# Projections stage: turns as 64-row tile pairs, four product banks, one query copy, no waiting additions

## The chip, the cores and the metric

One core of one Trainium2 chip runs the whole program. The metric is device time in microseconds (us) from the first to the last instruction; lower is better. The kernel before takes 2472.25 us (median of 3 runs, 2471.01 to 2472.43). TensorE is PE in the profile (PEld its weight loads), VectorE DVE, ScalarE ACT, GpSimd POOL, SyncE SP.

## The reference, cut to what matters

Two residual blocks on x (8 images, 256 channels, 64 by 64 pixels, float32). The change lies in the second one, in its projection `qkv` and in the sum `vk` over all pixels.

```python
x = x + _L0_conv_ref(_gn(x), ...)             # window mixing
# second block, on _gn(x):
qkv = einsum('bchw,oc->bohw', x, w_qkv)       # 768 output channels
y = conv5x5(qkv); y = conv1x1(y)              # a second set of 768
mqkv = concatenate([qkv, y]).reshape(B, -1, 24, N)
q, k, v = relu(first 8), relu(next 8), last 8 # per head
v = pad(v, ones row)
vk = einsum('bhdn,bhen->bhde', v, k)
out = einsum('bhde,bhen->bhdn', vk, q); out = out[:-1] / out[-1:]
x = x + batch_norm(einsum('bchw,oc->bohw', out, w_proj))
```

## The kernel before, in words

Four stages follow one another: window mixing, projections, convolved heads, output. Only `projections` is changed. It takes the images one by one, each in 8 chunks of 512 pixels (`n` from 0 to 7; 64 chunks in all). Images 0, 1, 6 and 7 are written out with constant wait values; images 2 to 5 run in a loop of two rounds, two images a round, and wait on values from registers (`over_image_pairs`). Below, "written-out" and "looped" chunks are these two kinds, 32 each.

A chunk on TensorE (`body` under `@block.tensor`):

- `product(b, n, j)` for j = 0 to 5 makes one tile of 128 output channels from six 128 by 128 by 512 matmuls (three float32r terms for two channel halves). j = 0 and 2 are the two key tiles, 1 and 3 the two value tiles, 4 and 5 the two query tiles. The products go round three PSUM banks, `o_ps[:, j % 3]`.
- `turn(b, n, u)` turns key tile and value tile of pair u (u = 0 after product 2, u = 1 after product 4) so that pixels lie on partitions: four 128 by 128 transposes each, keys into bank 0 of `t_ps`, values into bank 1. It first waits for four semaphores: that ScalarE has emptied the banks (`k_turned`, `v_turned`), and that the tiles lie in SBUF (`kv_ready`, `kv_ready_v`).
- `sum_vk(b, n, u)` for both u at the chunk's end adds value times key over the pixels: 16 small matmuls for each u, on tiles of 128 rows by 32 columns.
- In chunk n = 5, `means` and `variances` of the next image's normalization stand between the products.

The other engines in a chunk:

- ScalarE: `key(0)` copies product 0 out to `kv`; half of the next chunk's normalization; `key(1)`; `turned(0)`; the other half and the cast `xh`; the first query tile (`qw`, after product 4); `turned(1)`. A `turned` is two copies of 512 columns, `kT` and `vT`.
- VectorE: `value(n, 0)` copies product 1 out; pair differences into `stage` (`keys_values`); differences of the chunk before's queries; `value(n, 1)`; differences; `split` (the low part `xl` of the next chunk); the second query tile (L1314, after product 5); in chunks 1 to 4 a quarter of the next image's moments (`moments`), in chunk 4 also `gather`, whose result `means` waits for. The wait for product 1 is followed by three more semaphores (`cells_free`).
- GpSimd: for keys and values of each u and for queries `edge` and a copy into `stage`, then two ReLU passes of the queries into `qs`. After its waits and ahead of each `edge` it does a 128 by 1 addition into `tick` (`pause`), and so before `border`, a memset.
- SyncE stores `stage` and `qs` to DRAM as they get ready.

Semaphores that TensorE waits for before a product: j = 0 the second value copy and the first query copy of the chunk before; 1 the first query copy; 2 the second; 3 this chunk's first key copy; 4 the first value copy; 5 the second key copy.

In the next stage, `convolved_heads`, `turn` (L1572) is already made of 32-row tiles, in four banks, after small matmuls and ahead of a product. Its rows are read below for what such tiles cost.

Of the kernel before, what the change touches and what calls it, by code (L numbers as in the profile page):

```python
# [25 lines left out]
ALU = mybir.AluOpType  # L26
# [710 lines left out]
def projections(nc, K, x1_dram, qkv_dram, qr_dram, w_pw, bn_in, taps_dram, sorted_dram):  # L737
# [3 lines left out]
    with ExitStack() as ctx:  # L741
# [25 lines left out]
        vT = sb("vT", [P, 2, 4, NSQ, VS])  # L767
        tick = sb("ptick", [P, 4 * NCH])
# [6 lines left out]
        o_ps = psum("o_ps", [P, 3, 512])  # L775
        t_ps = psum("pt_ps", [P, 2, 512])
        vk_ps = psum("vk_ps", [P, 2, 512])
# [13 lines left out]
        kv_ready_v, q_ready_v = sem("kv_ready_v"), sem("q_ready_v")  # L791
# [5 lines left out]
        counted = sem("p_counted")  # L797

# [80 lines left out]
        def cells_free(eng, g):  # L879

            at_least(eng, t_full, 4 * (g - 1))
            at_least(eng, kv_diff, 2 * (g - 1))
            at_least(eng, kv_odd, 2 * (g - 1))
# [7 lines left out]
        def _(pool):  # L891
            pool.memset(vT[:, :, :, :, SQ:VS], 1.0).then_inc(zeroed, 1)

            def body(i, last_body):
                for par in range(2):
                    b = 2 * i + par

                    def pause(k, n):

                        k = NCH * k + n  # L900
                        pool.tensor_tensor(tick[:, k:k + 1], K["ident"][:, 0:1], K["ident"][:, 1:2], ALU.add)

                    def border(n):

                        row = NB * (1 - n // 4)
                        keys_values_free(pool, b, n)
                        queries_free(pool, b, n)
                        pause(0, n)
                        pool.memset(stage[:, n % 2, :, :, :, row, :].rearrange("p t a k x -> p (t a) k x"), 0.0)

                    def edge(buf, t0, j0, n):

                        if n % 2:
                            pool.tensor_scalar(staged(j0, n, 0, 0, 1), every_second(buf, t0, n, 0, 1), -1.0, None, ALU.mult)
                        else:
                            pool.tensor_copy(staged(j0, n, 1, HALF - 1, HALF), every_second(buf, t0, n, NB - 1, 1))

                    def keys_values(n, u):
# [4 lines left out]
                        pause(1 + u, n)  # L923
                        edge(kv, 2 * u, 2 * u, n)
                        pool.tensor_copy(staged(2 * u, n, 2), every_second(kv, 2 * u, n, 1 - n % 2)).then_inc(kv_odd, 1)

                    def queries(n, end=False):
                        g = NCH * b + n
                        pool.wait_ge(q_ready, g + 1)
                        pool.wait_ge(q_ready_v, g + 1)  # L930
                        queries_free(pool, b, n)
                        at_least(pool, K["qr_stored"][n % 2], 32 * (4 * b + n // 2))
                        pause(3, n)
# [8 lines left out]
                    for n in range(NCH):  # L942
                        if n % 4 < 2:
                            border(n)
# [8 lines left out]
        def _(act):  # L953
# [79 lines left out]
            def body(i, last_body):  # L1033
                for par in range(2):
                    b = 2 * i + par
                    for n in range(NCH):
# [5 lines left out]
                        def key(u):  # L1042
# [3 lines left out]
                            act.activation(kv[:, n % 2, 2 * u, :], o_ps[:, (2 * u) % 3, :], ACT.Copy).then_inc(kv_ready, 1)  # L1046

                        def turned(u):
                            act.wait_ge(t_full, 4 * g + 2 * u + 1)
                            at_least(act, vk_full, g)  # L1050
                            act.activation(kT[:, u, :, :].rearrange("p a c -> p (a c)"), t_ps[:, 0, :], ACT.Relu)\
                                .then_inc(k_turned, 1)
                            act.wait_ge(t_full, 4 * g + 2 * u + 2)
                            act.activation(vT[:, u, :, :, 0:SQ].rearrange("p a q c -> p (a q) c"),
                                           t_ps[:, 1, :].rearrange("p (a c) -> p a c", c=SQ), ACT.Copy).then_inc(v_turned, 1)
# [18 lines left out]
                        act.wait_ge(o_full, o0 + 5)  # L1074
                        queries_read(act, g)
                        act.activation(qw[:, n % 2, 0, :], o_ps[:, 1, :], ACT.Copy).then_inc(q_ready, 1)
                        turned(1)
                        if last_body and par == 1 and n == NCH - 1:
                            act.wait_ge(q_ready, g + 1)
                            act.wait_ge(q_ready_v, g + 1)  # L1080
# [18 lines left out]
        def _(pe):  # L1099
# [8 lines left out]
            pe.wait_ge(zeroed, 1)  # L1108

            def product(b, n, j):  # L1110
# [5 lines left out]
                if j == 0:  # L1116
                    at_least(pe, kv_ready_v, 2 * (NCH * b + n))
                    at_least(pe, q_ready, NCH * b + n)
                if j == 1:
                    at_least(pe, q_ready, NCH * b + n)  # L1120
# [1116 lines left out]
```

## Time and profile before

| | us |
|---|---|
| median of 3 runs | 2472.25 |
| lowest, highest | 2471.01, 2472.43 |
| span of the profiled execution | 2473.8 |
| first and last product matmul of the stage (L1132) | 266.9, 999.3 |

The profiled execution lies 1.5 us (0.06%) above the median. Starts are in us from the start of the span. A matmul's recorded time is its latency; matmuls are pipelined, so what a sequence costs is read from start to start.

### The profile page before, as it was taken

To read this page: it belongs to the slowest core of one execution; us is meant where nothing else is said; L and a number is where in the kernel's file an instruction comes from. 1 tells how busy PE (TensorE), PEld (TensorE's weight loads), DVE (VectorE), ACT (ScalarE), POOL (GpSimd) and SP (SyncE) were. 2 spreads that over 40 slices of the span, in tenths; PEclk is the share of its full clock that TensorE was granted. 3 is DMA by queue.
4 is the path that set the end of the run, shared out by engine and by line. 5 is a ranking of instruction groups with operands and counts; after the bars stand their busy time and mean duration, and the time that the engine had idled before them with its cause. 6 is when DMAs were issued, how large, how long until landed. Compare 5 with 4: busy or idle time off the path is not lost. (4 is left out here: it accounts for less than half of the span.)

```text
span 2473.8 us, 66794 instructions
## 1 busy us (share of the span) xinstructions
PE 2359.6 (95%) x25485; PEld 1881.3 (76%) x25485; DVE 1994.9 (81%) x2653; ACT 1495.6 (60%) x1864; POOL 1099.8 (44%) x1476
## 2 busy tenths in 40 slices
PE   5999799999999999799999999999999889999998
PEld 5889688877777887577888888888888656666666
DVE  7887688878788877778888888888888588888775
ACT  5777566666566666566776776677767434433442
POOL 7722387887787878200000000000000068888887
PEclk9999899999999999899999999999999999999999
DMA  7874689988988989988888888888888777777774
GB/s 285 336 301 173 208 295 344 329 293 314 316 288 323 344 299 302 253 196 207 209 209 208 209 210 207 210 208 209 207 208 210 228 243 280 275 275 271 271 272 136
DMA packets 300973, 628.38 MB, mean 254 GB/s; under 512 B 50784, under 2 KB 252256, under 8 KB 291552
## 3 DMA queue, kind: packets, MB, share of 16 engines
q1 hardware_dynamic: 295072, 590.38, 77.5%
q10 hardware_dynamic: 4688, 31.63, 3.6%
q0 software_dynamic: 1008, 3.67, 0.4%
q8 instruction: 125, 2.05, 0.3%
q14 instruction: 80, 0.66, 0.1%
HBM read 327.81 MB, written 300.94 MB: 254 GB/s over the span
## 5 line engine op out<-in xcount | busy, mean ns | idle before, releaser
L1562 PE MATMUL c_ps<-dh,wh 128*128 128x512 f32 x1152 | 465.3, 404 | 15.8 <-DVE wl L1712 9.9
L1477 ACT ACTIVATE dh<-image 128x1632 fp32r<-128x1632 f32 x192 | 301.5, 1570 | 269.9 <-PE c_ps L1562 254.8
L1562 PE MATMUL c_ps<-dh,wl 128*128 128x512 f32 x1152 | 456.4, 396 | 0.0
L1562 PE MATMUL c_ps<-dl,wh 128*128 128x512 f32 x1152 | 454.6, 395 | 1.6 <-issue 1.6
L1921 POOL TENSOR_TENSOR ql<-image,qh 128x1024 fp32r<-128x1024 f32 x1 | 2.4, 2359 | 967.8 <-DVE ql L2152 967.8
L1670 DVE TENSOR_TENSOR dl<-image,dh 128x1632 fp32r<-128x1632 f32 x192 | 356.3, 1856 | 73.9 <-ACT dh L1477 73.9
L1132 PE MATMUL o_ps<-xh,wqh 128*128 128x512 f32 x768 | 319.2, 416 | 11.3 <-issue 8.4
L1909 POOL TENSOR_TENSOR ql<-image,qh 128x1024 fp32r<-128x1024 f32 x126 | 300.9, 2413 | 10.7 <-ACT qh L1940 10.7
L1132 PE MATMUL o_ps<-xl,wqh 128*128 128x512 f32 x768 | 303.5, 395 | 0.0
L1132 PE MATMUL o_ps<-xh,wql 128*128 128x512 f32 x768 | 301.9, 393 | 0.0
L1562 PEld LDWEIGHTS c_ps<-dh,wh 128*128 128x128 f32 x1152 | 218.5, 190 | 68.6 <-DVE wl L1712 10.0
L1562 PEld LDWEIGHTS c_ps<-dl,wh 128*128 128x128 f32 x1152 | 218.2, 189 | 53.8 <-issue 1.3
L1562 PEld LDWEIGHTS c_ps<-dh,wl 128*128 128x128 f32 x1152 | 218.7, 190 | 46.1
L939 POOL TENSOR_SCALAR qs<-qw 128x512 f32<-128x512 f32 x126 | 239.1, 1913 | 0.0
L1046 ACT ACTIVATE kv<-o_ps 128x512 f32<-128x512 f32 x128 | 76.9, 601 | 255.8 <-PE o_ps L1132 246.0
L1961 ACT ACTIVATE zs<-z_ps,bn_shift 128x512 f32<-128x512 f32 x64 | 44.0, 687 | 278.2 <-PE z_ps L2048 278.2
L2048 PE MATMUL z_ps<-qh,fh 128*128 128x512 f32 x512 | 207.9, 406 | 3.1 <-issue 1.7
L2048 PE MATMUL z_ps<-qh,fl 128*128 128x512 f32 x512 | 200.1, 391 | 0.0
L2048 PE MATMUL z_ps<-ql,fh 128*128 128x512 f32 x512 | 199.8, 390 | 0.0
L1277 DVE COPY kv<-o_ps 128x512 f32<-128x512 f32 x128 | 87.9, 687 | 124.2 <-PE o_ps L1132 123.4
L973 ACT ACTIVATE xn<-image,p_nb,p_sc 128x512 f32<-128x512 f32 (+2 forms) x160 | 175.6, 1120 | 7.6 <-PEq L255 7.6
L1132 PEld LDWEIGHTS o_ps<-xh,wqh 128*128 128x128 f32 x768 | 145.8, 190 | 39.8 <-issue 14.2
(212 smaller groups left out, 5107.8 us busy)
## 6 DMA issues: line engine op xcount, KB each, us to landing
qkv_scratch<-stage SPq DMA_DIRECT2D x384, 408.0 KB, 4.7
image<-qkv_scratch SPq DMA_DIRECT2D x189, 816.0 KB, 6.3
yq_scratch<-qy SPq DMA_DIRECT2D x64, 512.0 KB, 6.7
image<-qr_scratch SPq DMA_DIRECT2D x128, 256.0 KB, 6.1
image<-yq_scratch SPq DMA_DIRECT2D x128, 256.0 KB, 5.3
ox<-x_scratch SPq DMA_DIRECT2D x8, 4096.0 KB, 15.3
qr_scratch<-qs SPq DMA_DIRECT2D x126, 256.0 KB, 3.6
out<-ox SPq DMA_DIRECT2D x7, 4096.0 KB, 12.7
```

Of the source, the lines that this page charges most:

```text
L939: last = pool.tensor_scalar(qs[:, n % 2, t, :], qw[:, n % 2, t, :], 0.0, None, ALU.max)
L973: last = act.activation(dst[:, :, to:to + rows, :], src[:, :, of:of + rows, :], ACT.Identity, bias=T["nb"][:, ct:ct + 1], scale=T["sc"][:, ...
L1046: act.activation(kv[:, n % 2, 2 * u, :], o_ps[:, (2 * u) % 3, :], ACT.Copy).then_inc(kv_ready, 1)
L1132: last = pe.matmul(o_ps[:, j % 3, :], w[:, ct, P * t:P * t + P], xx[:, n % 2, ct, :], start=(k == 0), stop=(k == 5))
L1277: dve.tensor_copy(kv[:, n % 2, 2 * u + 1, :], o_ps[:, (2 * u + 1) % 3, :]).then_inc(kv_ready_v, 1)
L1477: act.activation(dh[kind][:, :], raw[kind], ACT.Copy).then_inc(hi_ready, 1)
L1562: last = pe.matmul(c_ps[:, m, :], w[hp][:, kind, part, o:o + P], cells[:, :, HALF * dy:HALF * dy + HALF * NB], start=(k == 0), stop=(k == 5))
L1670: dve.tensor_tensor(dl[kind][:, :], raw[kind], dh[kind][:, :].bitcast(F32), ALU.subtract)\
L1909: pool.tensor_tensor(two_of(ql, n, tp), two(n, tp), two_of(qh, n, tp).bitcast(F32), ALU.subtract)\
L1921: pool.tensor_tensor(two_of(ql, 0, 1), two(0, 1), two_of(qh, 0, 1).bitcast(F32), ALU.subtract).then_inc(ql_ready, 2)
L1961: act.activation(zs[:, :], z_ps[:, 1, :], ACT.Identity, bias=bn["shift"][:, 1:2]).then_inc(z_taken, 1)
L2048: last = pe.matmul(z_ps[:, o, :], w[par][:, t, P * o:P * o + P], d, start=(m == 0), stop=(m == 3 * KT - 1))
```

## The change

`turn` becomes, for keys and values and each of four blocks, two transposes of 64 rows each: rows 0 to 63 into bank 0 and rows 64 to 127 into bank 1, so that keys take the first 256 columns of both banks and values the second 256. It raises `t_full` once, at its end, instead of after the keys and again after the values. Its four waits (`turn_ready`) move ahead of the last matmul of the product in front of it. `kT` and `vT` are read out with the two banks as one more dimension.

The products go round four banks, `(6n + j) % 4`; the two sums `vk` share one bank instead of two. ScalarE copies both query tiles in one activation of 1,024 columns after product 5 and after `turned(1)`; VectorE's copy of the second one is gone, and with it `q_ready_v` in all waits. Waits before products: j = 0 the second key copy of the chunk before, 1 the second value copy, 2 and 3 the query copy; 4 the first key copy of this chunk, 5 the first value copy. `pause` is gone on GpSimd; `edge` becomes a two-input operation with a zero; `border` comes after the first `edge`.

```diff
-            act.wait_ge(t_full, 4 * g + 2 * u + 1)
+            act.wait_ge(t_full, 2 * g + u + 1)
...
-        act.wait_ge(o_full, o0 + 5)
+        turned(1)
+        act.wait_ge(o_full, o0 + 6)
         queries_read(act, g)
-        act.activation(qw[:, n % 2, 0, :], o_ps[:, 1, :], ACT.Copy).then_inc(q_ready, 1)
-        turned(1)
+        act.activation(qw[:, n % 2, :, :], o_ps[:, bank(n, 4):bank(n, 4) + 2, :], ACT.Copy).then_inc(q_ready, 1)
...
+def product(b, n, j, before_last=None):
...
                 for w, xx in ((wh, xh), (wl, xh), (wh, xl)):
+                    if k == 5 and before_last:
+                        before_last()
...
-    for s in range(2):
+    for s, out in ((0, kt_ps), (1, vt_ps)):
         for a in range(4):
-            last = pe.transpose(t_ps[:, s, P * a:P * a + P], kv[:, n % 2, 2 * u + s, P * a:P * a + P], K["ident"][:, :])
-        last.then_inc(t_full, 1)
+            for r in range(2):
+                rows = slice(HALF_ROWS * r, HALF_ROWS * r + HALF_ROWS)
+                last = pe.transpose(out[:, r, HALF_ROWS * a:HALF_ROWS * a + HALF_ROWS],
+                                    kv[rows, n % 2, 2 * u + s, P * a:P * a + P], K["ident"][rows, rows])
+    last.then_inc(t_full, 1)
...
-                        product(b, n, 2)
-                        turn(b, n, 0)
+                        product(b, n, 2, lambda: turn_ready(b, n, 0))
+                        turn(n, 0)
...
-                        product(b, n, 4)
+                        product(b, n, 4, lambda: turn_ready(b, n, 1))
...
-                        dve.wait_ge(o_full, QT * g + 6)
-                        queries_read(dve, g)
-                        dve.tensor_copy(qw[:, n % 2, 1, :], o_ps[:, 2, :]).then_inc(q_ready_v, 1)
```

## Rows read from the trace of the kernel before

**Rows 1.** The page: each engine's busy time, share of the span and instructions.
```profile
PE 2359.6 (95%) x25485; PEld 1881.3 (76%) x25485; DVE 1994.9 (81%) x2653; ACT 1495.6 (60%) x1864; POOL 1099.8 (44%) x1476
```

**Rows 2.** Groups, 300 to 960 us: shapes, count, busy us, mean ns, idle before.
```profile
L1146 PE MATMUL pt_ps<-ident,kv 128*128 128x128 f32 x928 | 121.6, 274 | 5.3 <-DVE kv L1277 4.9
...
L901 POOL TENSOR_TENSOR ptick<-ident 128x1 f32<-128x1 f32 x204 | 87.4, 429 | 142.3 <-issue 63.1 <-DMA qkv_scratch<-stage 59.0 <-DVE kv L1277 20.2
...
L984 ACT ACTIVATE xh<-xn 128x1024 fp32r<-128x1024 f32 x57 | 60.5, 1061 | 1.9
...
L1314 DVE COPY qw<-o_ps 128x512 f32<-128x512 f32 x58 | 39.6, 683 | 2.9 <-PE o_ps L1132 2.4
```

**Rows 3.** Timeline of PE, one looped chunk: start, length, what, idle before.
```profile
610.64 0.47 PE L1132 MATMUL o_ps<-xh,wqh 128*128 128x512 f32 x1
...
614.39 0.39 PE L1132 MATMUL o_ps<-xh,wql 128*128 128x512 f32 x1
614.62 0.39 PE L1132 MATMUL o_ps<-xl,wqh 128*128 128x512 f32 x1
614.85 1.03 PE L1146 MATMUL pt_ps<-ident,kv 128*128 128x128 f32 x8
615.64 0.47 PE L1132 MATMUL o_ps<-xh,wqh 128*128 128x512 f32 x1
615.95 0.39 PE L1132 MATMUL o_ps<-xh,wql 128*128 128x512 f32 x1
...
618.26 0.39 PE L1132 MATMUL o_ps<-xl,wqh 128*128 128x512 f32 x1
...
620.86 0.76 PE L1158 MATMUL vk_ps<-vT,kT 128*32 128x33 f32 x64
621.82 0.47 PE L1132 MATMUL o_ps<-xh,wqh 128*128 128x512 f32 x1 [0.20 <-issue]
```

**Rows 4.** Timeline of PE in the convolved heads: product, small sums, 32-row turns, product.
```profile
1403.87 0.40 PE L1562 MATMUL c_ps<-dl,wh 128*128 128x512 f32 x1
1404.20 0.77 PE L1590 MATMUL yvk_ps<-yvT,ykT 128*32 128x33 f32 x64
1404.90 0.69 PE L1572 MATMUL yt_ps<-ident,vy 32*128 32x32 f32 x32
1405.42 0.67 PE L1572 MATMUL yt_ps<-ident,ky 32*128 32x32 f32 x32
1406.01 0.51 PE L1562 MATMUL c_ps<-dh,wh 128*128 128x512 f32 x1
1406.36 0.39 PE L1562 MATMUL c_ps<-dh,wl 128*128 128x512 f32 x1
```

**Rows 5.** Timeline of DVE, the value copies of the looped chunk in rows 3.
```profile
613.87 0.69 DVE L1277 COPY kv<-o_ps 128x512 f32<-128x512 f32 x1 [3.28 <-PE o_ps L1132]
...
617.66 0.68 DVE L1277 COPY kv<-o_ps 128x512 f32<-128x512 f32 x1
```

**Rows 6.** Timeline of PE, a written-out chunk: last matmul of product 2, chunk's end.
```profile
378.96 0.40 PE L1132 MATMUL o_ps<-xl,wqh 128*128 128x512 f32 x1
...
385.18 0.76 PE L1158 MATMUL vk_ps<-vT,kT 128*32 128x33 f32 x64
385.90 0.47 PE L1132 MATMUL o_ps<-xh,wqh 128*128 128x512 f32 x1
```

**Rows 7.** Timeline of DVE, the first value copy of that written-out chunk.
```profile
378.02 0.69 DVE L1277 COPY kv<-o_ps 128x512 f32<-128x512 f32 x1 [2.96 <-PE o_ps L1132]
```

**Rows 8.** Timeline of DVE: a value copy that comes late.
```profile
759.41 0.68 DVE L1277 COPY kv<-o_ps 128x512 f32<-128x512 f32 x1
```

**Rows 9.** Timeline of PE: the turn that waited for that copy.
```profile
760.24 1.07 PE L1146 MATMUL pt_ps<-ident,kv 128*128 128x128 f32 x8 [0.20 <-DVE kv L1277]
```

**Rows 10.** Timeline of PE, chunk 5: last matmul of product 1, then the means.
```profile
601.24 0.39 PE L1132 MATMUL o_ps<-xl,wqh 128*128 128x512 f32 x1
...
601.84 0.38 PE L161 MATMUL pstat_ps<-pmv,gavg 128*128 128x2 f32 x2 [0.22 <-DVE pmv L120]
```

More of the change, by code:

```diff
@@ L797, in projections, with bank @@
         counted = sem("p_counted")
+        def bank(n, j):
+            return (QT * n + j) % NO
         def image(i, par):
@@ L879, in cells_free @@
         def cells_free(eng, g):
-            at_least(eng, t_full, 4 * (g - 1))
+            at_least(eng, t_full, 2 * (g - 1))
             at_least(eng, kv_diff, 2 * (g - 1))
@@ L891, in _ @@
         def _(pool):
-            pool.memset(vT[:, :, :, :, SQ:VS], 1.0).then_inc(zeroed, 1)
+            pool.memset(zero[:, :], 0.0).then_inc(zeroed, 1)
+            pool.memset(vT[:, :, :, :, :, SQ:VS], 1.0).then_inc(zeroed, 1)
+            pool.wait_ge(zeroed, 2)
+            none = zero[:, :].unsqueeze(1).unsqueeze(2).broadcast_to([P, 4, NB, 1])
             def body(i, last_body):
@@ L922, in keys_values @@
                         keys_values_free(pool, b, n)
-                        pause(1 + u, n)
+                        if u == 0 and n % 4 < 2:
+                            queries_free(pool, b, n)
                         edge(kv, 2 * u, 2 * u, n)
+                        if u == 0 and n % 4 < 2:
+                            border(n)
                         pool.tensor_copy(staged(2 * u, n, 2), every_second(kv, 2 * u, n, 1 - n % 2)).then_inc(kv_odd, 1)
@@ L1107, in _ @@
                 last.then_inc(w_turned, 1)
-            pe.wait_ge(zeroed, 1)
-            def product(b, n, j):
+            pe.wait_ge(zeroed, 2)
+            def product(b, n, j, before_last=None):
                 t = TILES[j]
@@ L1131, in product @@
                     for w, xx in ((wh, xh), (wl, xh), (wh, xl)):
-                        last = pe.matmul(o_ps[:, j % 3, :], w[:, ct, P * t:P * t + P], xx[:, n % 2, ct, :],
+                        if k == 5 and before_last:
+                            before_last()
+                        last = pe.matmul(o_ps[:, bank(n, j), :], w[:, ct, P * t:P * t + P], xx[:, n % 2, ct, :],
                                          start=(k == 0), stop=(k == 5))
@@ L1135, in product, with turn_ready @@
                 last.then_inc(o_full, 1)
-            def turn(b, n, u):
+            def turn_ready(b, n, u):
                 at_least(pe, k_turned, 2 * (NCH * b + n) + u)
@@ L1143, in turn @@
                 pe.wait_ge(kv_ready_v, 2 * (NCH * b + n) + u + 1)
-                for s in range(2):
+            def turn(n, u):
+                for s, out in ((0, kt_ps), (1, vt_ps)):
                     for a in range(4):
-                        last = pe.transpose(t_ps[:, s, P * a:P * a + P], kv[:, n % 2, 2 * u + s, P * a:P * a + P],
-                                            K["ident"][:, :])
-                    last.then_inc(t_full, 1)
+                        for r in range(2):
[3 more added lines that the diff above has]
+                last.then_inc(t_full, 1)
             def sum_vk(b, n, u):
@@ L1157, in sum_vk @@
                         ch = slice(SQ * q, SQ * q + SQ)
-                        last = pe.matmul(vk_ps[ch, u, 0:VS], kT[:, u, a, ch], vT[:, u, a, q, :],
-                                         start=(n == 0 and a == 0), stop=(n == NCH - 1 and a == 3))
+                        last = pe.matmul(vk_ps[ch, u, 0:VS], kT[:, u, a, ch], vT[:, u, q // 2, a, q % 2, :],
+                                         start=(n == 0 and u == 0 and a == 0), stop=(n == NCH - 1 and u == 1 and a == 3))
                 if u == 1:
@@ L1276, in value @@
                             cells_free(dve, g)
-                        dve.tensor_copy(kv[:, n % 2, 2 * u + 1, :], o_ps[:, (2 * u + 1) % 3, :]).then_inc(kv_ready_v, 1)
+                        dve.tensor_copy(kv[:, n % 2, 2 * u + 1, :], o_ps[:, bank(n, 2 * u + 1), :]).then_inc(kv_ready_v, 1)
                     def keys_values(n, u):
```

56 lines of the change are left out of this document (22 added, 34 removed).

## The prediction

> **What bounds the kernel now.** I read the page first: TensorE is busy 95% of the span and no other engine over 81% [rows 1]. Busy time of pipelined matmuls says little, so I went to TensorE's timeline in the changed stage, from start to start. The reader is to see that nothing waits: product matmuls follow each other 0.23 us apart (614.39 to 614.62), the turn follows the last of them at the same 0.23, the next product follows the turn, and the chunk closes with the sums [rows 3]. One looped chunk is 11.18 us (from the first product's start at 610.64 to the next chunk's at 621.82). So in this stage each nanosecond that TensorE's sequence gets longer or shorter counts 64 times, and a saving on ScalarE, VectorE or GpSimd counts only where TensorE waits for it. Those places are few: idle time before all turns is 5.3 us in 660 us [rows 2], a fifth of a microsecond at a looped chunk's start marked "issue" [rows 3], and the means of chunk 5 [rows 10].
>
> **Part 1, the turn.** Before: the last product matmul starts at 614.62, the turn's first transpose at 614.85, the next product at 615.64, its second matmul at 615.95 [rows 3]. That is 1.33 us from the last matmul to the second one; without a turn two steps of 0.23 would lie there, so a turn costs 0.87. Eight transposes in 0.79 us are some 0.109 each (the last one's start to the product is about 0.03).
>
> After: the nearest rows are the turns of the convolved heads, with 32-row tiles [rows 4]. They show three prices.
> (a) Into a tiled stretch: from the last product matmul to the first tiled one 0.33 us (1403.87 to 1404.20), 0.10 more than the 0.23 inside a product. Nothing was waited for.
> (b) A block: the two turns start at 1404.90 and 1405.42, so 8 blocks take 0.52 us, 0.065 each as four 32-row tiles with 32 moving columns, against 0.109 as one tile of 128 rows with 128.
> (c) Out of it: the second turn's last block then starts at 1405.42 + 7 x 0.065 = 1405.87; the product starts 0.14 later (1406.01), against 0.03 after full transposes, and its second matmul 0.35 after that (1406.36), against 0.31. Together 0.15 more.
>
> A pair of 64-row tiles moves 64 columns. A straight line between the two rows of (b) gives 0.080 for it; its ends are 0.065 (the weight loads set the pace and the columns cost nothing) and 0.109 (the halves gain nothing). I take 0.080, since the pair differs from both rows in nothing but rows and columns per tile. Seven steps of 0.080 instead of 0.109 save 0.20; the drain of 64 columns instead of 32 takes about 0.01 more. A turn changes by +0.10 + 0.15 + 0.01 - 0.20 = +0.06, to the rows' hundredths; the start differences round up, and I take +0.05. For 128 turns **+6 us**. With 0.065 it is -0.05 a turn or -7 us, with 0.109 +0.26 or +33.
>
> The Trainium skill, "TensorEngine Tiling (Array Packing)", section Key Properties, says that changing the tiling mode drains TensorE; it speaks against short tiled turns between long products. (a) and (c), 0.25 a turn, agree with it; without it the same turns would give -25 us (rival 4).
>
> **Part 2, the waits moved ahead of a product's last matmul.** Queued behind them on TensorE are that matmul, the turn and everything after; the other engines all live on these products. The wait that ends last is VectorE's value copy. Where it holds a turn up, the turn starts 0.15 us after the copy's end: the copy ends at 760.09 and the turn starts at 760.24 [rows 8, 9]. A matmul held like that also pays its weight load in the open, 0.08 us (0.31 instead of 0.23 after a turn [rows 3]). So the last matmul is late by copy's end + 0.23 - its present start, if that is positive.
> Looped chunks, u = 0: the copy ends at 613.87 + 0.69 = 614.56, the matmul starts at 614.62 [rows 3, 5]: late by 0.17. 26 of the 28 looped chunks other than n = 5 look alike (copy's end -0.06 to +0.04 around the matmul's start); in chunk 5 the means leave room. 24 x 0.17 and 0.25 in the four first chunks are 5.1 us. The copy's own waits get one value fewer to work out (`t_full` now has the same as its neighbours), which may give up to 0.09 of it back; I take half, -1.3 us.
> Looped, u = 1: the copy ends at 618.34, the matmul starts at 618.26 [rows 3, 5], late by 0.31; but by then TensorE is 0.23 behind (0.17 and one turn), and VectorE's chain hangs on product 1, so about 0.08 is left in even chunks and nothing in odd ones: 1 us.
> Written-out chunks: the copy ends at 378.71, the matmul starts at 378.96 [rows 6, 7]: 0.25 of room for 0.23, so nothing, but with 0.02 to spare. Sum **+5 us**, with bounds 0 and +11 (written-out turns late by 0.05 each, +3; no relief at u = 1, 0.31 instead of 0.08 in twelve chunks, +3).
>
> **Part 3, the chunk's start.** From the sums to the product takes 0.96 us in the looped chunk (620.86 to 621.82, idle for "issue") and 0.72 in a written-out one [rows 3, 6]: 0.24 of register and wait instructions in TensorE's queue. Product 0 loses one of two waits. The 0.24 holds two or three such steps in the open, so one takes some 0.1 (an estimate): 32 x -0.1 = **-3 us**, between 0 and -6.
>
> **Part 4, the query copy.** VectorE loses 0.68 us a chunk [rows 2]. Its only use is chunk 4, where the moments come that much earlier: the means start 0.60 us after the last matmul instead of 0.23 [rows 10], and 0.37 of waiting goes, in seven chunks: **-2.6 us**. ScalarE's copy grows from 512 to 1,024 columns, 1.06 us by its cast of that size [rows 2]. Behind its wait for product 5 stand the next chunk's `key(0)` (due some 2.7 us later, two products' length) and the normalization; TensorE's product 2 and VectorE's differences need the queries later still. Hidden. `turned(1)` starts after the whole turn instead of after half, but without a query copy in front; two copies of 512 columns take about one of 1,024, so they end some 2 us after the turn starts, and the sums come 2.4 us after it (618.26 + 0.23 to 620.86 [rows 3]). Hidden, with 0.4 to spare.
>
> **Part 5, the rest.** Four banks: no product waits for a bank today, so nothing. The shared bank of the sums: nothing. GpSimd loses 204 additions of 0.43 us in 660 us [rows 2] and pays two-input edges; TensorE's releasers in these groups are VectorE and its own issue, not GpSimd [rows 2, 3], and SyncE gets its stores earlier. 59 of the 142 us of idle time before them are waiting for stores, which start no sooner by much: 0, with -3 as a bound for the few chunks where VectorE waits for a store too. The stage's end loses a pause of 0.43 and gains 0.38 of copy: 0.
>
> **Sum.** +6 + 5 - 3 - 2.6 = about +5 us. The profiled span of 2473.8 stands 1.5 over the median; the sum is made on differences and goes onto the median: **2477 us**.
>
> **Rivals.** (1) Faster: the weight loads alone set the pace of a pair. The rows cannot part load from columns in the 0.065; then the turns give -7 instead of +6, and with the copies 0.09 earlier part 2 gives +4: 2472 - 7 + 4 - 6 = 2463. It decides if a block takes under 0.073, where a turn costs what it does now. Against it: from 32 to 128 columns a block grows by 0.044. Chance 0.18.
> (2) The pair gains nothing, 0.109 a block: 2472 + 33 + 5 - 6 = 2504. Against it: four 32-row tiles do overlap [rows 4]. 0.07. The Trainium skill, "TensorE: Matmul & The Clock Gate", section LDWEIGHTS (loading the stationary operand), says that a load takes as long for 32 rows as for 128; if the sixteen loads of a turn went one after another, that rule would give this case.
> (3) Slower by the moved waits: they bite in the written-out images too, and u = 1 gets no relief, +11 instead of +5: 2483. For it: only 0.02 us of room [rows 6, 7]. 0.15.
> (4) The change does not do what it says: the 64-row turns run as before in the array's full mode, no switch is paid, but blocks still take 0.080: a turn loses 0.2, 2472 - 25 + 5 - 6 = 2446. Against it: [rows 4]. 0.05.
>
> **How the numbers follow.** My forecast's case has 0.55, its own range 2471 to 2483. The range is 2461 to 2488: it takes in rivals 1 and 3 and the bounds of parts 2 to 5, and leaves out 2 and 4 (0.12). A measurement of this kernel tells about 0.2% (4.9 us) from no change; the forecast lies at that edge, so its 0.55 is 0.27 slower, 0.27 same, 0.01 faster. Rival 1 adds 0.15 faster and 0.03 same, rival 2 0.07 slower, rival 3 0.14 slower and 0.01 same, rival 4 0.05 faster. Rounded: faster 0.21, same 0.31, slower 0.48.
>
> **What would show it.** In the profile after: last product matmul to first transpose 0.32 to 0.33; blocks 0.08 apart; 0.15 and 0.34 out of the turn; in looped chunks a gap of 0.40 instead of 0.23 ahead of product 2's last matmul, none in written-out ones; sums to product shorter by 0.1 in looped chunks; means 0.23 after the last matmul. I am wrong if written-out chunks get shorter (turn) or looped ones don't get longer by more than the written-out ones do (waits).

## The result, and the profile after

The changed kernel takes 2477.88 us (median; 2474.38 to 2482.05) against 2471.54 of the kernel before on the same chip: 1.0025 times, 95% interval 1.0015 to 1.0035, so some 6 us slower. The forecast was 2477. That the total came out is luck: the turns were forecast to cost 6 us and gain 6, and what the moved waits and GpSimd's program cost beyond the forecast makes up for that.

The page's first line of the changed kernel (as [rows 1]):

```profile
PE 2364.4 (96%) x26509; PEld 1842.6 (74%) x26509; DVE 1977.6 (80%) x2589; ACT 1545.0 (62%) x1864; POOL 1015.7 (41%) x1253
```

VectorE and GpSimd do less, ScalarE a little more, and TensorE's loads take less: sixteen half tiles for eight whole ones. Nothing of that is the time. TensorE's timeline of the same looped chunk as in [rows 3] (start, length, what):

```profile
613.07 0.49 PE L1131 MATMUL o_ps<-xh,wqh 128*128 128x512 f32 x1
...
616.81 0.39 PE L1131 MATMUL o_ps<-xh,wql 128*128 128x512 f32 x1
617.03 0.39 PE L1131 MATMUL o_ps<-xl,wqh 128*128 128x512 f32 x1
617.36 0.71 PE L1148 MATMUL pt_ps<-ident,kv 64*128 64x64 f32 x16
...
618.34 0.39 PE L1131 MATMUL o_ps<-xh,wql 128*128 128x512 f32 x1
...
620.41 0.39 PE L1131 MATMUL o_ps<-xh,wql 128*128 128x512 f32 x1
620.87 0.47 PE L1131 MATMUL o_ps<-xl,wqh 128*128 128x512 f32 x1
621.27 0.71 PE L1148 MATMUL pt_ps<-ident,kv 64*128 64x64 f32 x16
...
624.34 0.49 PE L1131 MATMUL o_ps<-xh,wqh 128*128 128x512 f32 x1
```

The chunk takes 11.27 us (613.07 to 624.34) against 11.18. At the first turn (u = 0) nothing waits: the last matmul stands 0.22 after the one ahead of it (616.81 to 617.03), the turn follows at 0.33, and from last matmul to second one of the next product it is 1.31 against 1.33. At the second (u = 1) the last matmul stands 0.46 behind (620.41 to 620.87): it waits for VectorE's second value copy. Before it stood 0.23 behind. The turn then follows after 0.40 instead of 0.32.

This is the pattern of the whole stage. Summed over the 64 chunks, start to start: the gaps ahead of product 4's last matmul give 18.0 us; against them stand the two turns with what is around them, -10.1 (part of it waits that stood behind the matmul before), the means -3.3 and the chunk starts -2.6. From the first product to the last chunk's start the stage takes 725.1 us against 720.5. Over all 64 chunks, to the last product's last matmul, it is 7.0 longer, so these four, +2.0 together, are not all: the other 5 are spread over steps inside products and the sums. Of them 1.4 are seven steps of the last chunk, at 0.43 us instead of 0.23: TensorE's granted clock is 0.57 there (994 to 998 us), for most of it the lower of its two levels (1.2 GHz), behind sums in which TensorE had sat idle for 1.62 us. In the kernel before it is 1.00 in that chunk.

Why the second value copy is late shows on VectorE. A written-out chunk (n = 1 of image 1, whose first value copy is [rows 7]) in the timeline of the kernel before, VectorE and then GpSimd:

```profile
378.81 0.63 DVE L1230 TENSOR_TENSOR stage<-kv 128x448 f32<-128x448 f32 x1
379.35 0.69 DVE L1232 TENSOR_TENSOR stage<-kv 128x512 f32<-128x512 f32 x1
379.95 0.68 DVE L1235 TENSOR_TENSOR stage<-qw 128x512 f32<-128x512 f32 x1
380.55 0.62 DVE L1236 TENSOR_TENSOR stage<-qw 128x448 f32<-128x448 f32 x1
381.65 0.69 DVE L1277 COPY kv<-o_ps 128x512 f32<-128x512 f32 x1 [0.48 <-PE o_ps L1132]
```
```profile
379.82 0.27 POOL L901 TENSOR_TENSOR ptick<-ident 128x1 f32<-128x1 f32 x1 [4.19 <-DMA qkv_scratch<-stage]
380.02 0.33 POOL L909 MEMSET stage<- 128x288 f32 x1
380.32 0.37 POOL L901 TENSOR_TENSOR ptick<-ident 128x1 f32<-128x1 f32 x1
380.65 0.90 POOL L914 TENSOR_SCALAR stage<-kv 128x64 f32<-128x64 f32 x1
381.42 0.64 POOL L925 COPY stage<-kv 128x512 f32<-128x512 f32 x1
```

The same chunk of the changed kernel, again VectorE and then GpSimd:

```profile
379.68 0.69 DVE L1279 COPY kv<-o_ps 128x512 f32<-128x512 f32 x1 [3.52 <-PE o_ps L1131]
380.46 0.63 DVE L1232 TENSOR_TENSOR stage<-kv 128x448 f32<-128x448 f32 x1
381.01 0.83 DVE L1234 TENSOR_TENSOR stage<-kv 128x512 f32<-128x512 f32 x1
381.76 1.13 DVE L1237 TENSOR_TENSOR stage<-qw 128x512 f32<-128x512 f32 x1
382.81 0.76 DVE L1238 TENSOR_TENSOR stage<-qw 128x448 f32<-128x448 f32 x1
383.49 0.68 DVE L1279 COPY kv<-o_ps 128x512 f32<-128x512 f32 x1
```
```profile
380.80 0.50 POOL L917 TENSOR_TENSOR stage<-zero,kv 128x64 f32<-128x64 f32 x1 [5.72 <-DMA qkv_scratch<-stage]
381.23 0.33 POOL L912 MEMSET stage<- 128x288 f32 x1
381.51 0.83 POOL L931 COPY stage<-kv 128x512 f32<-128x512 f32 x1
```

Before, the four differences follow each other 0.54 to 0.60 apart, and VectorE then waits 0.48 us for product 3. Beside them GpSimd does little: additions of one column, a memset, an edge. After, GpSimd's copy of 512 columns starts 1.83 us behind the start of VectorE's first value copy (379.68 to 381.51) instead of 3.40 (378.02 [rows 7] to 381.42), falls on the differences, and they take up to 1.05 (381.76 to 382.81). The wait for product 3 is gone because VectorE comes too late for it: first value copy to second 3.81 us against 3.63 [rows 7]. Only operations that read two tensors of SBUF get longer; the value copies stay at 0.68 or 0.69.

The Trainium skill, "SBUF — State Buffer", section "SBUF: two separate sides", says that a VectorE operation with two SBUF inputs and a GpSimd operation that reads SBUF share a pair of ports, which the one that comes first holds to its end. These rows agree with it: the 512-column query difference beside GpSimd's copy lasts 1.13 us instead of 0.68.

### The profile page after: what moved, and what is told of

It reads as the page before. It is cut to its first block and busy times, and to the rows that moved or that the text cites. A ratio compares the mean times of both kernels' runs of the same rounds, so it can differ in the third digit from the quotient of the medians.

```text
span 2475.7 us, 68153 instructions
## 1 busy us (share of the span) xinstructions
PE 2364.4 (96%) x26509; PEld 1842.6 (74%) x26509; DVE 1977.6 (80%) x2589; ACT 1545.0 (62%) x1864; POOL 1015.7 (41%) x1253
## 5 line engine op out<-in xcount | busy, mean ns | idle before, releaser
L1131 PE MATMUL o_ps<-xh,wqh 128*128 128x512 f32 x768 | 325.2, 423 | 8.2 <-issue 6.0
L1131 PE MATMUL o_ps<-xl,wqh 128*128 128x512 f32 x768 | 308.7, 402 | 11.5 <-DVE kv L1279 10.6
L943 POOL TENSOR_SCALAR qs<-qw 128x512 f32<-128x512 f32 x126 | 198.2, 1589 | 0.0
L1131 PEld LDWEIGHTS o_ps<-xl,wqh 128*128 128x128 f32 x768 | 145.9, 190 | 69.3 <-issue 32.6
```

What stands on the lines that cost most here:

```text
L943: last = pool.tensor_scalar(qs[:, n % 2, t, :], qw[:, n % 2, t, :], 0.0, None, ALU.max)
L1131: last = pe.matmul(o_ps[:, bank(n, j), :], w[:, ct, P * t:P * t + P], xx[:, n % 2, ct, :], start=(k == 0), stop=(k == 5))
```

## The experiments

Times are ratios to the kernel before on the same chip, and that ratio on 2472 us. "Waits" are summed over 62 chunks (chunks 2 and 63 wait for stores or a long chain in every kernel): what the step from a product's last matmul but one to the turn's first transpose is longer than unheld (0.46 us, with pairs 0.55). The last column counts chunks, of all 64, that wait over 0.06 us at u = 1. In seven chunks (n = 5) the variances' two matmuls stand in the step at u = 1. They add 0.11 to 0.14 us each time in every kernel, 0.8 to 1.0 us of that column, and these seven are counted even where nothing waits.

| kernel | ratio (95%) | us against before | waits u = 0, us | waits u = 1, us | chunks |
|---|---|---|---|---|---|
| before | | | 0.4 | 2.1 | 14 |
| changed | 1.0025 (1.0015, 1.0035) | +6.2 | 0.8 | 16.6 | 53 |
| pairs alone | 0.9976 (0.9967, 0.9985) | -5.9 | 0.0 | 2.5 | 12 |
| copy and banks alone | 0.9977 (0.9968, 0.9986) | -5.7 | 0.0 | 3.0 | 14 |
| waits ahead alone | 1.0031 (1.0020, 1.0042) | +7.7 | 5.5 | 3.3 | 20 |
| GpSimd alone | 1.0021 (1.0012, 1.0030) | +5.2 | 0.4 | 4.8 | 27 |
| waits ahead and GpSimd | 1.0064 (1.0052, 1.0076) | +15.8 | 6.1 | 14.4 | 53 |
| changed, waits behind | 0.9977 (0.9967, 0.9986) | -5.7 | 0.0 | 1.0 | 11 |
| changed, GpSimd of before | 0.9980 (0.9971, 0.9989) | -4.9 | 0.8 | 6.9 | 25 |
| changed, both undone | 0.9949 (0.9936, 0.9962) | -12.6 | 0.0 | 2.6 | 13 |

Without those seven chunks the counts are 7 before, 5 with pairs alone, 7 with copy and banks alone, 13 with waits ahead alone, 4 with the waits behind and 6 with both undone. In the other four kernels chunk n = 5 does wait, and the count stands.

The traces give a second measure, from one execution of each kernel: the stage from the first product to the last chunk's start, against 720.5 us before. In the order of the table it is +4.6, -3.1, -3.1, +7.0, +8.6, +17.5, -8.2, -2.2 and -9.6 us. The signs are those of the ratios; the sizes differ from them by up to 3.4. In the same executions the convolved heads, which no edit touches, take 935 to 943 us from their first product matmul to their last. So a difference of a few us between two kernels need not come from the edit.

My theory after the result: pairs and single copy gain, the moved waits and GpSimd's program lose, and these two make each other dear, since GpSimd makes the second value copy late and the moved waits take away the matmul that hid it. Rivals: the copies are late by themselves, GpSimd has no part in it, or pairs don't gain.

**1. Waits back behind the last matmul.**

```diff
-                        product(b, n, 2, lambda: turn_ready(b, n, 0))
+                        product(b, n, 2)
+                        turn_ready(b, n, 0)
                         turn(n, 0)
```

and so for u = 1. 

> The changed kernel with the turns' four waits back behind the product's last matmul, all else kept. (In looped chunks TensorE raises a semaphore between these waits and the first transpose, one more instruction in its queue.) Theory A: the waits ahead of the last matmul cost their time at u = 1 in nearly all chunks, because the second value copy now ends some 0.2 us too late for that matmul but not for the turn; the trace of the changed kernel holds 17.9 us of gaps ahead of product 4's last matmul and some 4 us more between that matmul and the turn, and 9.8 us of lateness that would stay behind it. So some 12 us go: 2478 - 12 = 2466 us, between 2464 and 2470 if the added instruction costs up to 0.06 in 64 looped turns; the gap ahead of product 4's last matmul is 0.23 everywhere. Theory B: the copies are late by themselves and the turn waits for them wherever the wait stands: 2476 to 2478 us, and the gap moves behind the last matmul.

Measured 0.9977; against the changed kernel some 12 us less, as theory A had it. In the written-out chunk above, the changed kernel and then this one (TensorE):

```profile
384.00 0.39 PE L1131 MATMUL o_ps<-xh,wql 128*128 128x512 f32 x1
384.32 0.47 PE L1131 MATMUL o_ps<-xl,wqh 128*128 128x512 f32 x1
```
```profile
384.17 0.39 PE L1131 MATMUL o_ps<-xh,wql 128*128 128x512 f32 x1
384.40 0.39 PE L1131 MATMUL o_ps<-xl,wqh 128*128 128x512 f32 x1
384.72 0.46 PE L1150 MATMUL pt_ps<-ident,kv 64*128 64x64 f32 x8
```

(The last view ends within the turn.) 0.32 becomes 0.23, and the turn still follows at 0.32: the copy was too late for the matmul and in time for the turn. The added semaphore instruction costs nothing that shows (0.319 in looped and written-out chunks alike).

**2. Pairs alone** (the kernel before with `turn` and `turned` as changed, waits as before).

```diff
-                        last = pe.transpose(t_ps[:, s, P * a:P * a + P], kv[:, n % 2, 2 * u + s, P * a:P * a + P],
-                                            K["ident"][:, :])
-                    last.then_inc(t_full, 1)
+                        for r in range(2):
+                            rows = slice(HALF_ROWS * r, HALF_ROWS * r + HALF_ROWS)
+                            last = pe.transpose(out[:, r, HALF_ROWS * a:HALF_ROWS * a + HALF_ROWS],
+                                                kv[rows, n % 2, 2 * u + s, P * a:P * a + P], K["ident"][rows, rows])
+                last.then_inc(t_full, 1)
```

> The kernel before with the turns as pairs of 64-row tiles alone (one t_full a turn, so the key copy waits for the whole turn; looped turns carry one more semaphore instruction). Theory A, from the trace of the changed kernel: a block takes 0.07 instead of 0.109, entry +0.09, exit +0.14, a turn and the product behind it 0.04 less: 128 x -0.04 = -5 us, 2471.5 - 5 = 2466.5, or up to 2470 with the added instruction; last matmul to first transpose 0.32, first to last transpose 0.49, then 0.15. Theory B, the forecast's term: 0.080 a block, +6 us: 2477.5.

Measured 0.9976, -5.9 us: theory A. The looped chunk of [rows 3], TensorE, and VectorE's first value copy:

```profile
614.67 0.39 PE L1133 MATMUL o_ps<-xl,wqh 128*128 128x512 f32 x1
614.99 0.71 PE L1151 MATMUL pt_ps<-ident,kv 64*128 64x64 f32 x16
615.63 0.50 PE L1133 MATMUL o_ps<-xh,wqh 128*128 128x512 f32 x1
615.96 0.39 PE L1133 MATMUL o_ps<-xh,wql 128*128 128x512 f32 x1
```
```profile
613.74 0.69 DVE L1282 COPY kv<-o_ps 128x512 f32<-128x512 f32 x1 [3.16 <-PE o_ps L1133]
```

1.29 us from last to second matmul instead of 1.33. The medians of all turns: entry 0.319 instead of 0.233, first to last transpose 0.489 instead of 0.763 (0.070 a pair instead of 0.109), out 0.152 and 0.335 instead of 0.028 and 0.314. Together -0.044, times 128 is -5.6 us. The 0.070 is a mean over a turn: by the single starts in the trace the two tiles of a pair start 0.003 apart, the second pair follows the first by 0.112, and from then on pairs follow each other by 0.061 to 0.064 (medians). The blocks of four 32-row tiles in the convolved heads do the same: 0.062 to 0.063 behind a first step of 0.084. And the value copy ends at 614.43, 0.24 before the last matmul, where it ended 0.06 before it [rows 3, 5]: with one `t_full` a turn, the copy's wait has a value that its neighbours have too, and 0.19 us of looped start-up are gone. Copy and banks alone has one `t_full` a turn too and shows the same, with full turns. In written-out chunks, whose wait values are constants, the copy starts as early in every kernel. That the register value is the reason is inferred from this; no run changes it alone.

**3. Waits ahead alone** (the kernel before, `turn_ready` ahead of the last matmul, full turns).

```diff
-                        product(b, n, 4)
+                        product(b, n, 4, lambda: turn_ready(b, n, 1))
```

and so for u = 0. 

> The kernel before with the turns' waits moved ahead of the last product matmul alone. Theory A: the price of moved waits depends on how late the value copies are, and in the kernel before they are late mainly in looped chunks; by its trace (a held matmul starts 0.15 after the copy's end) 3.6 us at u = 0 in looped chunks, 6.6 at u = 1 in written-out and 4.2 in looped ones, of which 7.9 are paid behind the matmul already: +6.5, 2471.5 + 6.5 = 2478 us, and gaps at u = 0 in looped chunks. Theory B: u = 1 is held in nearly all chunks whatever the other engines do, as in the changed kernel: +12 to +14, 2484 us.

Measured 1.0031, +7.7 us; theory A said +6.5. The waits are where the forecast had put them, at u = 0 in looped chunks (VectorE, then TensorE):

```profile
617.10 0.69 DVE L1280 COPY kv<-o_ps 128x512 f32<-128x512 f32 x1 [3.11 <-PE o_ps L1134]
```
```profile
617.62 0.39 PE L1134 MATMUL o_ps<-xh,wql 128*128 128x512 f32 x1
617.94 0.47 PE L1134 MATMUL o_ps<-xl,wqh 128*128 128x512 f32 x1
618.24 1.03 PE L1149 MATMUL pt_ps<-ident,kv 128*128 128x128 f32 x8
```

The copy ends at 617.79, the matmul starts 0.15 later, and the turn 0.30 after that instead of 0.23: 0.17 a chunk. At u = 1 20 chunks are counted (13 without the seven named above), not 53.

**4. GpSimd alone** (the kernel before with GpSimd's changed program).

```diff
-                        pause(1 + u, n)
                         edge(kv, 2 * u, 2 * u, n)
+                        if u == 0 and n % 4 < 2:
+                            border(n)
...
-                            pool.tensor_copy(staged(j0, n, 1, HALF - 1, HALF), every_second(buf, t0, n, NB - 1, 1))
+                            pool.tensor_tensor(staged(j0, n, 1, HALF - 1, HALF), every_second(buf, t0, n, NB - 1, 1), none, ALU.add)
```

> The kernel before with GpSimd's program of the changed kernel alone (no waiting additions, edges as two-input operations, border behind the first edge). Theory A: GpSimd's copies start earlier and run beside VectorE's query differences, which get longer (from some 0.7 to 1.1 us each), so VectorE's second value copy comes 0.1 to 0.2 later; the turns' waits stand behind the last matmul, which hides it except where the copy is late already: 0 to +2 us, 2471.5 to 2473.5. Theory B: GpSimd has nothing to do with it; start to start of VectorE's two value copies stays at 3.67 us in written-out chunks.

Measured 1.0021: theory A's mechanism at a higher price, 5.2 us instead of up to 2. The chunk shown above has the query differences of the changed kernel and no wait of VectorE for product 3 (VectorE's timeline):

```profile
384.73 1.13 DVE L1230 TENSOR_TENSOR stage<-qw 128x512 f32<-128x512 f32 x1
385.79 0.75 DVE L1231 TENSOR_TENSOR stage<-qw 128x448 f32<-128x448 f32 x1
386.46 0.68 DVE L1272 COPY kv<-o_ps 128x512 f32<-128x512 f32 x1
```

I had counted on the last matmul to hide it. In written-out chunks it does; in looped ones the copy comes 0.27 us later than before and 0.14 shows. The split of `xl` grows too, from 1.28 to 1.58 us on the mean. The waits at u = 1 grow by 2.7 us (table), so they are only part of the 5.2; in the trace some 1.9 us more lie between product 5 and the next chunk and 1.0 at the means.

**5. GpSimd of before in the changed kernel** (the diff of 4 turned round, nothing else). 

> The changed kernel with GpSimd's program of the kernel before (waiting additions, one-input edges, border first), waits still ahead of the last matmul. Against the kernel before on the same chip (taken as 2472). Theory A: the second value copies come 0.15 to 0.2 earlier again, and the waits at u = 1 hold only the chunks in which the copy is late anyway (9.8 us by the trace of the pairs alone, against 17.9 of gaps and 4 behind them now): the change's +6 becomes -4, 2468 us; gap ahead of product 4's last matmul 0.23 in most chunks. Theory B: the lateness comes from the waits and the query copy, not from GpSimd: 2476 to 2478.

Measured 0.9980, -4.9 us, theory A (25 chunks wait instead of 53).

**6. Both undone** (the edits of 1 and 5 together). 

> Both undone: waits behind the product's last matmul and GpSimd's program of the kernel before; what is left of the change is the pairs, the single query copy and the banks. Before taken as 2472. Theory A (parts add up): pairs -6 and the forecast's parts 3 and 4, -3 and -2.6: 2461 us. Theory B (the GpSimd program costs nothing once the waits stand behind): as with the waits alone moved back, 2465 to 2466.

Measured 0.9949, theory A: 2461.65 us by its own median, 2459.4 by the ratio on 2472; faster than both kernels. What is left of the change is pairs, one query copy and four banks.

**7. Copy and banks alone** (as 6, and the turns full, with one `t_full` each):

```diff
-                        for r in range(2):
-                            rows = slice(HALF_ROWS * r, HALF_ROWS * r + HALF_ROWS)
-                            last = pe.transpose(out[:, r, HALF_ROWS * a:HALF_ROWS * a + HALF_ROWS],
-                                                kv[rows, n % 2, 2 * u + s, P * a:P * a + P], K["ident"][rows, rows])
+                        last = pe.transpose(t_ps[:, s, P * a:P * a + P], kv[:, n % 2, 2 * u + s, P * a:P * a + P],
+                                            K["ident"][:, :])
```

> Only what is left beside pairs, moved waits and GpSimd: one ScalarE copy for both query tiles, four banks, the sums in one bank, the waits ahead of products 0 to 5. Before taken as 2472. Theory A (parts 3 and 4 of the forecast): 2466.5; sums to product 0.25 instead of 0.35 in looped chunks, means 0.4 to 0.5 earlier in seven chunks. Theory B (single runs so far: pairs -6, waits +8, GpSimd +5, the whole change +6, which leaves -1): chunk 5 gives its gain back at the second turn and little is left, 2471.

Measured 0.9977, -5.7 us (some 2.2 either way): theory A. Sums to product is 0.238 instead of 0.352 in looped chunks (medians), and chunk 5's waits for the means fall from 4.5 to 1.1 us over seven chunks.

**8. Query differences late.** The changed kernel with one move on VectorE:

```diff
-                        if n > 0:
-                            queries(n - 1)
...
                         if nxt and n == 6:
                             scale()
+                        if n > 0:
+                            queries(n - 1)
```

> The changed kernel, with VectorE's differences of the queries of the chunk before moved from ahead of the second value copy to the chunk's end (behind the split and the moments). Waits and GpSimd as changed. Before taken as 2472. Theory A: the second turn waits because VectorE's chain between its two value copies has become longer than two products and a turn; with 1.4 to 1.9 us out of that chain no copy is late, the 18 us of gaps ahead of product 4's last matmul and the 4 behind them go nearly all, chunk 5's among them: 2478 - 20 = 2458 us. Theory B: the copy is late for another reason (product 3, ScalarE's copies): 2476 to 2478. Theory C: the differences, now late, hold the moments, the next chunk's first value copy or a store: gaps appear at u = 0 or at chunk starts, 2465 or more.

Measured 1.0018 (1.0008 to 1.0028), about +4.4: my price fell, its mechanism didn't, and theory C took what it freed. In the median chunk, looped and written-out, nothing waits at u = 1 any more (0.23 ahead of the matmul). But 6.8 us of waits come up at u = 0, above all in chunk 5 (VectorE, then TensorE):

```profile
331.19 2.46 DVE L111 BATCH_NORM_STATS2 pbst<-image 128x6 f32<-128x512 f32 x4
...
334.77 1.14 DVE L1234 TENSOR_TENSOR stage<-qw 128x512 f32<-128x512 f32 x1
335.84 0.68 DVE L1279 COPY kv<-o_ps 128x512 f32<-128x512 f32 x1
```
```profile
335.65 0.40 PE L1131 MATMUL o_ps<-xh,wql 128*128 128x512 f32 x1
336.66 0.47 PE L1131 MATMUL o_ps<-xl,wqh 128*128 128x512 f32 x1 [0.61 <-DVE kv L1279]
```

The moments and the late differences push the next chunk's first value copy out. Chunks 2, 42, 50 and 57 wait longer too, together 4.8 us more than in the changed kernel; for these I did not follow the chain to its start.

**9. Additions back.** Changed kernel, waits behind, and on GpSimd only the addition ahead of each edge:

```diff
+                        pause(1 + u, n)
                         edge(kv, 2 * u, 2 * u, n)
```

> The changed kernel with the waits behind the last matmul and, on GpSimd, the waiting addition back ahead of each edge; the two-input edges and the border behind the first edge stay as changed. Before taken as 2472. With the waits behind alone it was 0.23% below the kernel before, with GpSimd's whole program of before too 0.51% below. Theory A: what GpSimd's change costs is the time at which its copies and passes start, and the addition in front sets that: 2460 to 2462 us, the split of xl back from 1.62 to some 1.25 us, second value copy no later than the last matmul. Theory B: the two-input edges (0.56 to 0.75 us) or the border's place cost it: 2465 to 2467.

Measured 0.9961 (0.9948 to 0.9975), -9.6 us, a little over half of the way from -5.7 (no additions) to -12.6 (GpSimd's whole program of before). The interval reaches the second and nearly the first, so the times alone don't give the additions' share; that they carry most of GpSimd's price is argued from the rows that follow, and what two-input edges add is not shown. In the chunk above VectorE waits for product 3 again (its timeline), and the split is short again in the groups of 300 to 960 us (count, busy us, mean ns, idle before; the changed kernel, then this one):

```profile
381.25 0.69 DVE L1291 COPY kv<-o_ps 128x512 f32<-128x512 f32 x1 [0.43 <-PE o_ps L1139]
```
```profile
L1226 DVE TENSOR_TENSOR xl<-xn,xh 128x1024 fp32r<-128x1024 f32 x58 | 94.1, 1622 | 0.0
```
```profile
L1238 DVE TENSOR_TENSOR xl<-xn,xh 128x1024 fp32r<-128x1024 f32 x59 | 73.1, 1239 | 0.0
```

**10. Additions twice** (as 6, and in `pause`):

```diff
-                        pool.tensor_tensor(tick[:, k:k + 1], K["ident"][:, 0:1], K["ident"][:, 1:2], ALU.add)
+                        for s in range(2):
+                            pool.tensor_tensor(tick[:, 2 * k + s:2 * k + s + 1], K["ident"][:, 0:1], K["ident"][:, 1:2], ALU.add)
```

> Waits behind the last matmul and GpSimd's program of the kernel before, with two additions in place of each one: the suspected effect doubled. Before taken as 2472; with one addition 2459.6 by its ratio. Theory A: GpSimd's start matters only as far as its copies meet VectorE's chain to the second value copy; one addition takes them out of it, a second adds nothing: 2458 to 2461 us. Theory B: still later is still better: below 2457. Theory C: GpSimd, busy 44% of the span, becomes late for the first copies of the next chunk (they wait for its copies of two chunks before) or for stores: above 2463.

Measured 0.9981 (0.9972 to 0.9990), -4.7 us: theory C by its number, 8 us worse than with one. The second value copy does come earlier still (0.04 us in the median chunk), so its lateness isn't the price; the split grows again, to 1.43 us. Of the 8 us the stage's trace shows 2.4 up to the last chunk's start. 5.4 lie in the convolved heads (942.6 against 937.2 us), whose program is the same in both, and within what that stage differs by among the executions. So theory C's reason is not shown.

**11. Halves apart.** Pairs alone, with the loop over halves outside:

```diff
-                    for a in range(4):
-                        for r in range(2):
+                    for r in range(2):
+                        for a in range(4):
```

> The pairs alone, as run before (-0.24%), but in each turn the four transposes of rows 0 to 63 follow each other first and then the four of rows 64 to 127, so that neighbours use the same half of the array. Before taken as 2472. Theory A: a pair takes 0.070 us because its two halves work side by side, and a tile by itself takes about what a whole block takes, 0.065 or more: first to last transpose 1.0 us instead of 0.49, 128 turns for keys and values: 2466 + 65 = 2531 us. Theory B: a 64-row tile of 64 columns costs 0.035 by itself and its neighbour doesn't matter: 0.49 again, 2466 us.

Measured 1.0002 (0.9992 to 1.0012). TensorE, a turn and its neighbours:

```profile
615.44 0.39 PE L1133 MATMUL o_ps<-xl,wqh 128*128 128x512 f32 x1
615.76 0.76 PE L1151 MATMUL pt_ps<-ident,kv 64*128 64x64 f32 x16
616.45 0.50 PE L1133 MATMUL o_ps<-xh,wqh 128*128 128x512 f32 x1
```

Theory A is out by a factor of ten: first to last transpose is 0.537 (median), not 1.0. By the total it is nearly theory B: 0.036 a tile on the mean of a turn, 0.033 when the halves take turns. But by the single starts the tiles come in twos here too: 0.007 to 0.017 apart in a two, then 0.061 to 0.064 from one two to the next, but for a first step of 0.112 and one of 0.103 (medians). The trace does not tell a tile's half. So it stays open whether two neighbours on one half go like this or TensorE still worked on both halves side by side, and what a 64-row tile costs by itself is not shown. The 0.05 a turn that the alternating order saves is 6 us of 128 turns, and that is all that pairs alone had gained.

**12. Waits ahead and GpSimd together** (the kernel before with the diffs of 3 and 4). 

> The kernel before with two parts of the change together: waits ahead of the last matmul and GpSimd's changed program. Alone they cost 0.31% and 0.21%. Before taken as 2472. Theory A (each makes the other dear: GpSimd makes the second value copy late, the moved waits take away the 0.23 us that hid it): more than the sum, 2472 + 7.7 + 5.2 + 4 = 2489 us; in the trace nearly all chunks wait at u = 1. Theory B (they add up): 2485 us; by the trace no more chunks wait at u = 1 than with either alone (20 and 27). The times are only 2 us apart on either side of 2487; the count of chunks decides.

Measured 1.0064, +15.8 us, where +7.7 and +5.2 make +12.9. By the time alone (+12.9 to +18.7) the sum isn't excluded; by the count it is theory A: 53 chunks wait at u = 1, as in the changed kernel, and 14.4 us against 3.3 and 4.8. So that the two meet is shown in the waits; the time points the same way within its intervals.

## Why the prediction was right, and where it was not

The parts alone make -5.9 - 5.7 + 7.7 + 5.2 = +1.3 us; the whole change makes +6.2. The 4.9 between them I put down to what moved waits and GpSimd do to each other: each of these figures has an interval of some 2.3 either way, so the times alone don't prove it, and by the stage's length in the traces the four parts make +9.4, more than the whole (+4.6). Taken two by two, the sign is steadier: together the moved waits and GpSimd cost 2.9 more than apart in the kernel before (experiment 12) and 4.2 more in the changed kernel (from both undone, +7.7 and +6.9 alone and +18.8 together), by the stage's length 1.9 and 5.4 more. The count of waiting chunks (53 with both, 13 and 27 with one, the seven of n = 5 counted only where they wait) does show that there is such a thing; the size of its price stays open. The forecast made it +6 + 5 - 3 - 2.6 + 0. The turns came out 12 us better; the moved waits (2.7), GpSimd (5.2) and those 4.9 came out 12.8 worse. No step of the forecast foresaw this balance.

**Part 1 (+6, measured -6).** Entry (+0.10, measured +0.09) and exit (+0.15, measured +0.14) were right, and agree with the drain of the Trainium skill, "TensorEngine Tiling (Array Packing)", section Key Properties. The mis-sized term is the block: I drew a straight line in columns between 32-row and 128-row tiles and took 0.080; it is 0.070, close to the row of the convolved heads (0.065), and rival 1's condition (under 0.073) was met. Behind the first step of a turn both kinds of block take 0.062: going from 32 to 64 moving columns cost nothing, so the line was no model, and the end of the range at which "the columns cost nothing" was the right one. Rival 2's condition, loads one after another at a whole tile's price, did not come: a pair takes 0.062, one 128-row tile 0.109. The rule named there is that a load takes as long for 32 rows as for 128 (the Trainium skill, "TensorE: Matmul & The Clock Gate", section LDWEIGHTS). The runs don't settle it: blocks with loads of 32 and of 64 rows take the same 0.062, which agrees; the 128-row block takes 0.109, but it also moves 128 columns.

**Part 2 (+5, measured +7.7 alone).** The price of a held matmul (copy's end + 0.15, then 0.08 more in the open) was right, and so was its place, in the kernel before: experiment 3 shows 0.17 at u = 0 in looped chunks. In the changed kernel that place is empty. The step that failed is "I take half, -1.3 us" for the register value that `t_full` no longer needs: it gave 0.19 us, not 0.045, and the copy got out of the way. What came instead is rival 3's "they bite in the written-out images too", at u = 1, for a reason that neither names.

**Part 5 (0, measured +5.2 alone, and more with the moved waits).** This step was wrong. I asked who waits for GpSimd and found nobody, and left out whom GpSimd's operations slow down when they move. The reason given, "TensorE's releasers in these groups are VectorE and its own issue, not GpSimd", held the hint: what delays VectorE's chain delays TensorE.

**Parts 3 and 4 (-3 and -2.6)** measured -5.7 together. In the changed kernel the means do start 0.23 after the last matmul, as forecast ([rows 10] has 0.60):

```profile
603.77 0.39 PE L1131 MATMUL o_ps<-xl,wqh 128*128 128x512 f32 x1
604.00 0.28 PE L161 MATMUL pstat_ps<-pmv,gavg 128*128 128x2 f32 x2
```

but chunk 5 hands back more than that at u = 1, where it now waits 0.6 to 1.1 us, 5.2 in its seven chunks (the variances' matmuls not counted).

**The two signs named for being wrong:** looped chunks had to get longer by more than written-out ones; both grew by 0.09 us (medians 11.13 to 11.22, 10.96 to 11.05). That sign alone said that part 2's place was wrong, under a total that was right to 1 us. The other sign, written-out chunks that get shorter, did not come up although the turns did get cheaper: the waits at u = 1 covered it. With the waits behind, written-out chunks take 10.84.

## What to carry to other kernels

An operation that looks like idle padding can be a spacer: before taking it out, lay the two engines' operations over each other at the new start times and ask which pairs read SBUF side by side. A wait is worth what lies between it and the need; moving one ahead of a matmul spends that matmul's length as slack, and two changes that each fit into the same 0.23 us of slack do not fit together. When a total comes out as forecast, check the terms by their places.

## What the runs showed of the hardware that was not expected

- Behind the first step of a turn, a block turned as two 64-row tiles takes 0.062 us, as much as one turned as four 32-row tiles (0.062); as one tile of 128 rows it takes 0.109. A switch into half tiles and back costs 0.09 and 0.14 us.
- VectorE's operations with two SBUF inputs take up to 1.05 us start to start instead of 0.60 beside GpSimd copies, its copies from PSUM 0.69 in any case.
- With one `t_full` a turn, so that a wait's register value is one that its neighbours have too, a looped VectorE copy starts 0.19 us earlier; that it is the value is inferred.
